# Norm rows fetched during routing, four buffers for rows of experts, and every block of the output written by GpSimd's indirect DMA

## The reference

```
L0:  x = x + strength(sample) * response(x)
L1:  h = styled layer norm of x;  each token goes to its 2 best of 8 experts:
     y = sum over its 2 experts of gate * (relu(h @ w1[e] + b1[e]) @ w2[e] + b2[e]);  x = x + y
L2:  each sample has one of 8 experts e2 (an input):
     o = gelu(x @ Wi[e2] + bi[e2]) @ Wo[e2] + bo[e2];  r = o + x
     y = (r - mean) * rsqrt(var + 1e-12) * gamma2[e2] + beta2[e2]
L3:  y is rotated in groups of four features by the sample's angles
```

## Time and profile before

| | |
|---|---|
| three runs | 384.92 us median (383.84 to 384.99) |
| the profiled execution | 380.56 us, of which the span of instructions is 378.8 us |
| PE busy | 233.9 us (62%) |
| DVE busy | 173.4 us (46%) |
| ACT busy | 129.3 us (34%) |
| POOL busy | 127.8 us (34%) |
| TensorE clock granted, mean | 0.85 of full speed |

### The profile page before, as it was taken

How to read it: one execution, slowest core, us unless ns; L and a number is a source line. 1 busy time by engine, 2 the same in 40 slices (tenths; PEclk the granted TensorE clock), 3 DMA queues, 4 the chain that set the end, 5 groups by cost and what they waited for, 6 DMA issues and landing times.

```text
span 378.8 us, 6313 instructions
## 1 busy us (share of the span) xinstructions
PE 233.9 (62%) x1440; PEld 192.8 (51%) x1440; DVE 173.4 (46%) x682; ACT 129.3 (34%) x390; POOL 127.8 (34%) x189
## 2 busy tenths in 40 slices
PE   2247788637524699676766699676465656666520
PEld 1035544623514388676655699235364656655520
DVE  4607874789639554323333355023334332352550
ACT  2203455363122256334433365024131222343310
POOL 5755500042014574222222240274334413010151
PEclk9999999956555799989999999989885665798975
DMA  1299200000022024435443443434333222241100
GB/s 32 46 315 338 83 2 1 0 0 3 0 83 54 16 73 113 106 94 109 104 97 92 110 105 95 122 74 123 87 81 99 59 87 75 58 120 60 27 28 5
DMA packets 37192, 30.07 MB, mean 79 GB/s; under 512 B 7474, under 2 KB 29788, under 8 KB 37156
## 3 DMA queue, kind: packets, MB, share of 16 engines
q1 hardware_dynamic: 31588, 18.97, 18.8%
q0 software_dynamic: 2976, 5.97, 6.1%
q10 hardware_dynamic: 2592, 4.72, 4.7%
HBM read 23.54 MB, written 5.05 MB: 75 GB/s over the span
## 4 chain that ended last, share of the span: by engine, by line
PE 23%; DMA 20%; DVE 17%; SPq 16%; issue 9%; POOL 8%; ACT 2%; ACTq 2%; POOLq 0%; DVEq 0%
DMA expert_rows<-es 11%; PE bank L986 6%; DMA big<-in_x_dram,mapx 5%; PE bank L1047 5%; SPq L386 4%; PE bank L891 2%; ACTq L727 2%; POOL big L591 2%; SPq L391 2%; SPq L380 2%; SPq L377 2%; SPq L384 2%; SPq L427 2%; DMA big<-expert_rows,sloti 1%; PE bank L1044 1%
## 5 line engine op out<-in xcount | busy, mean ns | idle before, releaser
L578 POOL DMA_INDIRECT hg<-h_rows,map x39 | 36.9, 947 | 63.9 <-PE bank L982 57.8
L986 PE MATMUL bank<-hgT,ws 128*128 128x128 f32 x312 | 44.1, 285 | 22.3 <-DVE hgT L1350 22.3
L986 PEld LDWEIGHTS bank<-hgT,ws 128*128 128x128 f32 x312 | 38.6, 195 | 27.1 <-DVE hgT L1350 26.8
L740 ACT ACTIVATE hid<-bank,bh 128x128 f32<-128x128 f32 x78 | 24.4, 363 | 61.6 <-PE bank L986 61.5
L1006 PE MATMUL bank<-w,hid 128*128 x312 | 42.3, 280 | 0.1
L591 POOL DMA_INDIRECT big<-expert_rows,sloti x32 | 31.1, 973 | 25.1 <-DMA expert_rows<-es 16.2
L1368 DVE TENSOR_TENSOR es<-bank,b2blk 128x128 f32<-128x128 f32 x39 | 11.4, 292 | 60.8 <-DMA expert_rows<-es 57.2
L1006 PEld LDWEIGHTS bank<-w,hid 128*128 128x128 f32 x312 | 38.7, 195 | 0.4 <-issue 0.3
L986 PE MATMUL bank<-hg,ws 128*128 128x128 f32 x176 | 31.7, 339 | 11.0 <-DMA hg<-big 11.0
L986 PEld LDWEIGHTS bank<-hg,ws 128*128 128x128 f32 x176 | 28.9, 249 | 12.2 <-DMA hg<-big 12.2
L1403 DVE BATCH_NORM_STATS2 st<-bank 128x6 f32<-128x128 f32 x22 | 6.6, 299 | 62.0 <-PE bank L1047 62.0
(11 more groups left out here) (321 smaller groups left out, 407.7 us busy)
## 6 DMA issues: line engine op xcount, KB each, us to landing
ws<-in_L_cond_Wi_dram ACTq DMA_DIRECT2D x18, 256.0 KB, 2.7
b2blk<-in_L_cond_exp_b_dram SPq DMA_DIRECT2D x39, 64.0 KB, 3.2
expert_rows<-es SPq DMA_DIRECT2D x39, 64.0 KB
w<-in_L_cond_exp_w_dram SPq DMA_DIRECT2D x1, 2048.0 KB, 11.0
gb<-in_L_cond_gamma_dram SPq DMA_DIRECT2D x22, 64.0 KB, 2.7
gb<-in_L_cond_beta_dram SPq DMA_DIRECT2D x22, 64.0 KB, 3.1
hg<-big SPq DMA_DIRECT2D x22, 64.0 KB, 2.3
h_rows<-big SPq DMA_DIRECT2D x4, 256.0 KB, 2.2
```

Of the source, the lines that this page charges most:

```text
L578: pool.indirect_dma_start(out=hg[:, b % RING, :], out_offset=None, in_=hdram, in_offset=bass.IndirectOffsetOnAxis(ap=map1[:, b:b + 1], axi ...
L740: last = act.activation(hid[:, u, c, :], ps[2 + u][:, c * P:(c + 1) * P], ACT.Relu, bias=bh1[:, c, b:b + 1])
L986: last = mm(ps[2 + 2 * (c // 2) + u][:, c % 2 * P:(c % 2 + 1) * P], ws[:, w, c * P:(c + 1) * P], rows, start=True, stop=True)
```

## The change

Three things are moved.

- `norm_rows(j)` for all 22 blocks leaves the first expert loop and stands on SP behind the loads of the start, ahead of the four stores of `hrow`, behind a wait for `oh88_ready`.
- `es` has four buffers in place of two, each with a semaphore of its own. `x2` moves into free columns of `big` and `gelu0` into a tile of its own, which makes room.
- `SCATTERED` is 22: SP's `out_of_block` goes, with its 64 DMAs and 64 register loads, and POOL writes all 22 blocks with `rows_out`. The twelve scatters of blocks 0 to 11 stand in POOL's queue behind `power(6)` and ahead of `power(7)`; two more stand behind each later `power`.

```diff
-        es = sb("es", [P, 2, D])
+        es = sb("es", [P, RING, D])
...
-        gelu0 = big[:, 4 * NT - D - 2:4 * NT - D]
-        x2 = sb("x2", [P, RING, D])
+        gelu0 = sb("gelu0", [P, 2])[:]
+        x2 = big[:, YF + 10 * D:YF + 14 * D].rearrange("p (j d) -> p j d", d=D)
...
-        SCATTERED, OUT_LAG = 6, 6
+        SCATTERED = 22
...
-        es_stored = [sem(f"es_stored{i}") for i in range(2)]
+        es_stored = [sem(f"es_stored{i}") for i in range(RING)]
...
+            def norm_rows(j):
+                e = sp.value_load(bex2i[0:1, j:j + 1], min_val=0, max_val=E - 1)
+                for k, rows in enumerate((gamma2, beta2)):
+                    sp.dma_start(gb[:, j, k, :],
+                                 rows[bass.ds(e, 1), :].rearrange("e d -> (e d)").partition_broadcast(P)).then_inc(gb_ready, 16)
+
+            sp.wait_ge(oh88_ready, 1)
+            for j in range(NB2):
+                norm_rows(j)
+
             for g in range(GROUPS):
                 sp.wait_ge(hrow_sb, g + 1)
...
-                sp.dma_start(edram[b * P:(b + 1) * P, :], es[:, r % 2, :]).then_inc(es_stored[r % 2], 16)
+                sp.dma_start(edram[b * P:(b + 1) * P, :], es[:, r % RING, :]).then_inc(es_stored[r % RING], 16)
...
                 if b + RING < NB1:
                     bias_rows(b + RING, r)
-                if 2 <= b < NB2 + 2:
-                    norm_rows(b - 2)
...
             for j in range(NB2):
                 rows_in(j, j % RING)
-                if 0 <= j - OUT_LAG < NB2 - SCATTERED:
-                    out_of_block(j - OUT_LAG)
-            for j in range(NB2 - OUT_LAG, NB2 - SCATTERED):
-                out_of_block(j)
-            sp.wait_ge(yo_stored, 16 * SPT * (NB2 - SCATTERED))
             sp.wait_ge(last_stored, 16 * SCATTERED)
...
-            pool.wait_ge(es_stored[0], 16 * ((NB1 + 1) // 2))
-            pool.wait_ge(es_stored[1], 16 * (NB1 // 2))
+            for r in range(RING):
+                pool.wait_ge(es_stored[r], 16 * len(range(r, NB1, RING)))
...
             for m in range((TILES - 4) // 2, NB2 // 2):
                 power(m)
-                if m - 1 >= (NB2 - SCATTERED) // 2:
+                if m == (TILES - 4) // 2:
+                    for j in range(2 * m):
+                        rows_out(j)
+                else:
                     rows_out(2 * m - 2)
                     rows_out(2 * m - 1)
...
-                if b >= 2:
-                    dve.wait_ge(es_stored[u], 16 * (b // 2))
-                dve.tensor_tensor(es[:, u, :], ps[6 + u][:, 0:D], b2blk[:, r % RING, :], ALU.add).then_inc(es_ready, 1)
+                if b >= RING:
+                    dve.wait_ge(es_stored[r % RING], 16 * (b // RING))
+                dve.tensor_tensor(es[:, r % RING, :], ps[6 + u][:, 0:D], b2blk[:, r % RING, :], ALU.add).then_inc(es_ready, 1)
```

More of the change, by code:

```diff
@@ L251, in cond_seq_kernel @@
         hgb = sb("hgb", [P, 2, P])
+        YF = 3 * NT + P
         x2a = big[:, 4 * NT - D:4 * NT]
-        gelu0 = big[:, 4 * NT - D - 2:4 * NT - D]
-        x2 = sb("x2", [P, RING, D])
+        gelu0 = sb("gelu0", [P, 2])[:]
+        x2 = big[:, YF + 10 * D:YF + 14 * D].rearrange("p (j d) -> p j d", d=D)
         st2, mv2 = sb("st2", [P, 6]), sb("mv2", [P, RING, 2])
         ve2, rs2 = (sb(n, [P, RING]) for n in ("ve2", "rs2"))
-        YF = 3 * NT + P
         yn = big[:, YF:YF + RING * D].rearrange("p (j d) -> p j d", d=D)
@@ L419, in rows_in @@
                 sp.dma_start(hg2[:, r, :], x2T[:, bass.ds(c, P)]).then_inc(hg2_ready[r], 16)
[L421 to L428, removed]
             sp.wait_ge(cst2_ready, 1)
```

## The result

On the chip of the first comparison the changed kernel takes 347.07 us (median of four runs, 344.8 to 348.38) against 384.38 us for the kernel before (four runs, 379.06 to 384.99). The ratio is 0.909, with a 95% interval of 0.895 to 0.923: faster by 9%. The forecast was 351 us, with a range of 344 to 361. The profiled execution took 348.38 us, of which the span is 346.6.

What follows compares the result with a forecast made beforehand. SP's queue was taken to bound the first expert loop, then PE. Span 378.8 - 29.8 - 3.9 = 345.1 us, 346.9 with 1.8 around it, and 351 by the 1.1% from profile to median; range 344 to 361.

Steps and rivals of the forecast that it cites:

- The loop: First expert loop: with norm rows gone and four buffers, PE paces it at 1.89 us, 29.8 us less (28 to 30.8).
- the two have one answer: First expert loop: norm rows out and four buffers taken together, since two buffers alone would still bind at times.
- Rival A: First expert loop: some hidden cycle binds at a pace between, say 2.3 us; price 15.6 us, time 367; chance 0.08.
- The norm rows in their new place: SP before the `hrow` stores: 35 us of issues fit into waiting time, cost 0, with 0 to 1 us for disturbance.
- Rival D: Norm rows hold SP past its deadline before the `hrow` stores, making the kernel slower, up to 428 us; chance 0.01.
- another time from the last `es` to the last combine: Second stage: a changed time from the last L1368 to the last combine would show the prediction wrong; no size given.
- The tail on the first chip: From `power(6)` on: POOL's 22 scatters and five powers take 33.2 us, 3.9 us less (0 to 5).
- The caution about the clock: Behind `power(6)`: at half clock PE's blocks would take 3.9 us in place of 2.1, leaving a gain of 1 to 2.
- The close: POOL's closing DRAIN: 7.7 us after the last scatter, unchanged; 1.3 more if growing with all indirect DMAs, at most 20.5 more.
- The step from the profile to the median: Whole kernel: the median lies 1.1% above the profiled execution, as before, so 346.9 us gives 350.9.
- rival C: Tail and close: scatters wait for DVE, 10 us more, or the close grows by up to 20.5; time 361 to 371; chance 0.09.
- rival B: Second stage: the granted clock falls or rises otherwise, 8 us more or less, time 359 or 343; chance 0.09.

Runs made afterwards that it cites:

- p1: Kernel before, with only the norm rows moved out of the loop, two `es` buffers kept: 356.93 us, ratio 0.916.
- p2: Kernel before, with only four `es` buffers and the moves of `x2` and `gelu0`, norm rows still in the loop: 384.81 us, ratio 0.989.
- r4: Changed kernel with 16 more early gathers by POOL whose result is not used: 370.07 us, ratio 0.957 to the kernel before.
- p3: Kernel before, with only the output of all 22 blocks written by POOL: 394.41 us, ratio 1.015.
- q1: The changed kernel run again on chip 5, against the kernel before there: 362.51 us, ratio 0.931.
- p4: Kernel before, with norm rows moved and four buffers, output as before, on chip 13: 355.64 us, ratio 0.915.
- q2: Norm rows moved and four buffers, output as before, beside the changed kernel on chip 5: 356.13 us, ratio 0.917 to the kernel before.
- r2: Norm rows moved and four buffers, output as before, run once more on chip 5: 356.35 us, ratio 0.917 to the kernel before.
- q3: Changed kernel with scatters spread, two behind each power from `power(2)`, four between `power(6)` and `power(7)`: 350.35 us, ratio 0.901 to the kernel before.
- r1: The changed kernel run once more on chip 5, against the kernel before there: 361.44 us, ratio 0.930.
- q4: Changed kernel with scatters spread and SP's store issued ahead of the second-stage weights: 349.48 us, ratio 0.898 to the kernel before.

## Why the prediction was right, and where it was not

**The loop.** Predicted: -29.8 us (28 to 30.8), paced by PE at 1.89 us. Measured: -31.2, at 1.87 us. The mechanism stands, and is shown by p1 and p2: taking the norm rows off SP gives nearly all of it, and buffers without that give 2.7 us. That "the two have one answer" was an overstatement: with two buffers the loop loses only 1.8 us, for ten waits that PE mostly absorbs, and its first gather follows the last `es` 1.2 us sooner. Rival A, a pace between, fell: no wait for a store is left.

**The norm rows in their new place.** Predicted: 0, between 51 and 87 us, the first store of `hrow` near 110. Measured: 51.35 to 86.3, and 109.55. Rival D fell. r4 adds a condition that I had not seen. SP's round, which the prediction took from rows where POOL issued one gather at a time, is not kept beside a burst: one gap there is 7 us long, and SP is done with the norm rows at 98.2 us and not at 86.3. Half of the cover of 24 us would be gone by it.

**The stretch behind the last `es`.** Predicted: no change, by a sum without a term for it; the prediction named another time from the last `es` to the last combine as a sign of being wrong. Measured: +2.4 us to the first gather. The last combine begins 88.5 us behind the last `es` against 87.7, so 1.6 us of it are made good by then, and 2.3 us are there again at `power(6)`. What failed is a step of the loop's part: I took SP as free once PE bounds, and did not ask what stands in SP's queue ahead of the last store. In the kernel before that queue's lateness was hidden in DVE's wait for one of two buffers.

**The tail on the first chip.** Predicted: POOL's queue of 22 scatters and 5 powers, 33.2 us, and 3.9 us less. Measured: 33.15, and 4.0 less. DVE waited 8.9 us for `power(7)`, where 8 were predicted, and PE 7.9 behind it. The caution about the clock was met in part: behind that wait PE's down products took 1.91 us against 1.06, as in the earlier trace rows for the up product, but POOL stayed the later of the two and the gain stayed whole:

```profile
314.38 1.06 PE L1038 MATMUL bank<-wo,hid 128*128 x8
...
324.77 1.91 PE L1038 MATMUL bank<-wo,hid 128*128 x8
```

**The tail on the later chips.** Here the term has the wrong sign: on chip 5, 37.0 to 37.5 us became 39.3 to 40.1, and p3 on chip 13 has 40.5. The count of instructions is that of the first chip; what was added is three late results of PE, 14.6 us in q1, partly under cover of POOL's burst. No rival of the prediction was of this kind. In microseconds the 361.44 and 362.51 us of chip 5 lie just outside the range, 344 to 361; but the kernel before is slower there as well, and as a ratio 0.930 and 0.931 lie inside 344 / 384.92 to 361 / 384.92, which is 0.894 to 0.938.

**The close.** Predicted: 7.7 us unchanged, with +1.3 if it grew with the total of indirect DMAs. Measured: +1.3, one of the prediction's own signs of being wrong. That the number fits the total is luck, for r4 shows that the rule behind it is not the right one: 16 early gathers added 0.3. The bound of +20.5 was far off.

**The step from the profile to the median.** This is the largest miss. The parts gave a profiled time of 346.9 us, and 348.38 was measured: 1.5 us off, where the parts not foreseen, +2.4 and +1.3, were partly made up by the loop, -1.4, and by the start, -0.7, for which there was no term. The prediction then added 1.1%, 4.0 us, because the median of the kernel before lay that far above its profiled execution. With the changed kernel the median lies 1.3 us below it. Nearly all of the 3.9 us between 351 and 347.07 comes from carrying that ratio over; it belonged to the one execution that was profiled, not to the kernel. The number came out right within 1.1% although this step had the wrong sign.

**The scatters beside DVE (rival C).** They took 980 to 1223 ns, 1036 in the mean, against 974 to 1085 in the earlier trace rows: 22 x 0.05 us is 1 us in all, so rival C's 10 us did not come. The eight scatters beside which DVE does nothing take 0.980 to 0.982 us, the others 0.982 to 1.223, so work on DVE costs a scatter 0.24 us at most. By the exclusive lock of the Trainium skill, SBUF — State Buffer, "Who interferes with whom", they would have waited for DVE's rotation. A wait behind the whole of it, some 2 us for each pair, is not there, which agrees with the section's own inference, that descriptor generation needs only the write side; what the small excess is, no run shows.

**The second stage's clock (rival B).** From the first gather to `power(6)` 91.0 us against 91.1: unchanged on the first chip, and over its last 66 us the granted clock is 0.69 in both kernels. On the later chips it varies from 91.5 to 98.0 us between p1, p2, p4, q2 and r2, which do not differ there; p1, the longest, has a late result of 6.4 us in its burst of `gather_y`.

**What stays open.** Why a result of PE comes late beside a burst of POOL's indirect DMAs. r4 shows that such a burst brings it about, and in q3 a shorter one brings less. The granted clock does not explain it: in q1 it is 1.00 over the first late result and 0.50 over the third.

```profile
317.00:322.00 5.00, 0.97 (x9) 0.78 (x7) 2.00 (x7) 0.69 (x3) 3.78 (x5) 1.00 0.11 36
322.00:328.00 6.00, 3.16 (x16) 2.87 (x16) 0.00 (x0) 0.45 (x2) 4.78 (x5) 0.61 0.33 96
328.00:334.00 6.00, 0.77 (x2) 0.50 (x2) 1.82 (x8) 1.56 (x6) 3.05 (x5) 0.50 0.07 25
```

Nor is the DMA traffic high there, with shares of 0.07 to 0.33. Whether PE itself stands, or what it waits for in its queue, the records do not tell, since ends of matmuls are modelled. In r4 SP's issues stall in the same burst, so it need not be a matter of PE alone; a common cause was not tested. Why the first chip's traces show none of it is open too: they are only two. Open as well are the 1.7 and 4.3 us by which the changed kernel is late at `power(6)` in r1 and q1 against the kernel without the output part.

## What to carry to other kernels

When an engine waits for a DMA, look at the turn of that DMA in its queue before adding buffers: here moving 44 small transfers into idle time of SP gave 30 us, and the buffers alone under 3. When the bound moves off a queue, or more buffers take a wait away, look at that queue's last item again, because its lateness was hidden until then. Before giving POOL a burst of indirect DMAs, spread them: the same 22 scatters, most of them two at a time, made a tail of 26.4 us out of one of 39 to 40 on the same chip. And don't carry the distance between one profiled execution and the median from one kernel to the next.

## What the hardware showed that I had not expected

- Waits of ACT and DVE for results of PE with no recorded releaser, only beside indirect DMAs that POOL issues back to back (41 of more than 2 us in twelve of fourteen traces; the longest, in r4, 12.5 us, for a result 10.1 us behind the modelled end of the matmul).
- In r4's burst SP's own DMA issues slow down too: 4 in place of 18 in 14.6 us, with one gap of 7.0 us.
- POOL's closing DRAIN: 10.4 us with 93 indirect DMAs, 11.3 to 11.4 with 109, and 11.5 with 125, where the 16 added were early gathers.
- The last store of 64 KB lands 3.0 to 3.8 us after its issue when a load of 256 KB is issued just ahead of it (before, changed, p1, p2, q3), and 4.6 us in q4, where one more such load follows it 1.2 us later; putting it first brings nothing.
